# Layer 1's dt product from stacked half-precision halves, and the experts' middle one slot later

## What is computed

```
proj = hidden @ W_in.T;  x, gate = split(proj)           # 1024 channels each
x = silu(causal_conv(x, 4 taps))
ssm = x @ W_x.T;  ts, B, C = split(ssm, [32, 16, 16]);  each one RMS-normalised
dt = softplus(ts @ W_dt.T + b_dt)                        # the product that changes
state = state * exp(dt * A) + (dt * x) * B               # scan over the tokens, 16 states
y = (sum over states of state * C + x * D) * silu(gate)
x = x + ga * (y @ W_out.T)
# experts: base = h @ base_W.T; mid = (h @ lora_A) * w_top2; x = x + gb * (base + 2 * mid @ lora_B)
```

## Time and profile before

| | |
|---|---|
| median of three runs | 1513.37 us (1512.45 to 1514.31) |
| profiled execution, its own time | 1512.44 us |
| its span | 1510.3 us |
| PE, DVE, ACT, POOL busy share | 89%, 80%, 63%, 68% |
| instructions | 25293 |
| layer 1 in the span | from 489 us on |
| an iteration of layer 1 | 118.1 us |

### The profile page before, as it was taken

How to read it: one execution, slowest core, us unless ns; L and a number is a source line. 1 busy time by engine, 2 the same in 40 slices (tenths; PEclk the granted TensorE clock), 3 DMA queues, 4 the chain that set the end, 5 groups by cost and what they waited for, 6 DMA issues and landing times.

```text
span 1510.3 us, 25293 instructions
## 1 busy us (share of the span) xinstructions
PE 1349.8 (89%) x8817; PEld 1006.2 (67%) x8817; DVE 1213.1 (80%) x1643; ACT 952.1 (63%) x2617; POOL 1028.2 (68%) x697
## 2 busy tenths in 40 slices
PE   6899999999999959699899899899899999988677
PEld 5566677768776748568668667667766766855543
DVE  5794674556443469999999999999999999999994
ACT  3432343233321577788888897798798888886761
POOL 0353242313212398998998999899899899899870
PEclk9799999999999979899999999999999999999689
DMA  9531222101100200100110110020030020020001
GB/s 331 195 112 37 91 79 84 56 29 36 36 29 15 87 18 1 57 29 15 57 42 1 57 57 1 31 83 1 15 99 1 15 86 14 1 71 29 1 1 42
DMA packets 32388, 77.16 MB, mean 51 GB/s; under 512 B 3667, under 2 KB 4723, under 8 KB 31750
## 3 DMA queue, kind: packets, MB, share of 16 engines
q1 hardware_dynamic: 32262, 75.55, 15.1%
HBM read 66.99 MB, written 8.55 MB: 50 GB/s over the span
## 4 chain that ended last, share of the span: by engine, by line
PE 31%; POOL 13%; DVE 12%; ACT 6%; issue 5%; DVEq 0%; ACTq 0%; POOLq 0%
PE ps_h L1502 10%; DVE h L2273 7%; POOL h L2131 7%; POOL dbu L2097 6%; PE ps_m L1466 4%; DVE acc L2289 3%; ACT ps_a L1757 2%; PE ps_o L1526 2%; PE ps_m L165 2%; PE ps_s L1466 2%; PE ps_m L166 2%; PE ps_m L167 2%; PE ps_m L1426 2%; ACT ab L1889 1%; PE ps_s L165 1%
## 5 line engine op out<-in xcount | busy, mean ns | idle before, releaser
L2273 DVE TENSOR_TENSOR_SCAN h<-ps_a,dbu 128x512 f32<-128x512 f32 x512 | 595.8, 1205 | 21.3 <-ACT ps_a L1757 7.1
L2097 POOL TENSOR_TENSOR dbu<-dtu,b_all 128x1020 f32<-128x1020 f32 x256 | 598.3, 2358 | 14.4 <-DVE h L2273 13.9
L1757 ACT ACTIVATE ps_a<-dt,a_neg 128x256 f32<-128x256 f32 (+1 forms) x1024 | 442.9, 466 | 67.7 <-DVE h L2273 66.6
L1502 PE MATMUL ps_h<-ident,h 128*128 128x128 f32 x1536 | 226.4, 290 | 65.3 <-DVE acc L2289 60.0
L2289 DVE SCALAR_TENSOR_TENSOR acc<-ps_h,c_cur,acc 128x512 f32<-128x512 f32 x384 | 267.9, 737 | 16.9 <-PE ps_h L1502 16.3
L1502 PEld LDWEIGHTS ps_h<-ident,h 128*128 128x128 f32 x1536 | 183.1, 149 | 123.0 <-DVE h L2273 82.4
L724 POOL TENSOR_TENSOR hid_l<-hid,hid_h 128x256 f16<-128x256 f32 (+1 forms) x88 | 77.4, 883 | 155.0 <-ACT hid_h L610 154.8
L2131 POOL TENSOR_TENSOR h<-h,c_all 128x1024 f32<-128x1024 f32 x64 | 151.1, 2362 | 19.2 <-ACT carry L1777 19.2
L602 ACT ACTIVATE sil<-ps_gu 128x256 f32<-128x256 f32 (+1 forms) x88 | 33.9, 385 | 180.6 <-PE ps_gu L167 180.6
L165 PE MATMUL ps_m<-h_h,wi_h 128*128 128x256 f16 x432 | 119.4, 276 | 2.6 <-PEq L155 2.4
L166 PE MATMUL ps_m<-h_l,wi_h 128*128 128x256 f16 x432 | 119.2, 276 | 0.0
(11 more groups left out here) (406 smaller groups left out, 2876.8 us busy)
## 6 DMA issues: line engine op xcount, KB each, us to landing
b_all<-bt_scratch SPq DMA_DIRECT2D x32, 512.0 KB, 3.9
wm<-in_wmod SPq DMA_DIRECT2D x7, 1024.0 KB, 5.2
wo<-in_wmod SPq DMA_DIRECT2D x5, 1024.0 KB, 8.6
xa<-in_x SPq DMA_DIRECT2D x8, 512.0 KB, 4.5
stage<-in_W_in SPq DMA_DIRECT2D x4, 1024.0 KB
x_scratch<-x SPq DMA_DIRECT2D x8, 512.0 KB, 3.1
c_all<-bt_scratch SPq DMA_DIRECT2D x8, 512.0 KB, 6.0
x<-x_scratch SPq DMA_DIRECT2D x8, 512.0 KB, 3.6
```

Of the source, the lines that this page charges most:

```text
L1502: tr = pe.transpose(ps_h[:, t, j * P:(j + 1) * P], h[:, s % RING, j, t * P:(t + 1) * P], W["ident"][:])
L1757: ex = nc.scalar.activation(ps_a[:, j, j % 2:], dt[:, m, j % 2:], ACT.Exp, scale=a_neg[:, m, st:st + 1])
L2097: nc.gpsimd.tensor_tensor(dbu[:, s % AHEAD, :, 1:], dtu[:, :, 1:], b_all[:, st, 1:].unsqueeze(1).to_broadcast([P, DG, CH - 1]), ALU.mult). ...
L2273: nc.vector.tensor_tensor_scan(h[:, s % RING, two].rearrange("p j t -> p (j t)"), ps_a[:, two].rearrange("p j t -> p (j t)"), dbu[:, s % A ...
```

## The change

dt's product is made in half precision. Both factors are split in a high and a low half and stacked on the contraction axis: `w_dt` (scaled by WS = 64) has rows high, high, low of W_dt and high, low of b_dt; `ts` has rows high, low, high and ones. One half-precision matmul of 128x256 then gives the three products that the single-precision one stood for. For this `ssn` holds ts three times (`rms_apply` writes 192 instead of 64 elements), ACT copies all three to `ts` in slot 23, PE takes the high half from the middle rows in PSUM (`low_of_ts`, a new matmul by `minus_mid`, slot 23), and ACT copies the rest in slot 24: the low half, B and C to `tsb`, and `b0` (`ts_low_in`). So `spread_b` waits for a copy one slot later. The dt tiles stand four in slot 24 and four in slot 26, `dt_abs` takes four tiles in slot 25 and four in slot 27. `MID_AT` goes from 27 to 28 and `LB_AT` from 29 to 30. Before the loop, `w_dt` is made on chip: five DMAs instead of three, two ACT copies and one DVE operation more, and ACT's load of the table for ln moves behind `ts_low_in`.

```
-DT_AT = {23: (0, 1), 24: (2, 3), 25: (4, 5), 26: (6, 7)}
-MID_AT = 27
+DT_AT = {24: (0, 1, 2, 3), 26: (4, 5, 6, 7)}
+MID_AT = 28
-LB_AT = {29: (0, 1)}
+LB_AT = {30: (0, 1)}
...
-            pe.matmul(dt_bank(m), w_dt[:, m * P:(m + 1) * P], tsb[:], start=True, stop=True)\
+            pe.matmul(dt_bank(m), w_dt[:, m * P:(m + 1) * P], ts[:], start=True, stop=True)\
...
+        def low_of_ts(n):
+            pe.wait_ge(S["ts_done"], n * 2 + 1)
+            pe.matmul(ps_s[:, 0:CH], minus_mid[:], ts[:], start=False, stop=True, skip_group_check=True).then_inc(S["ts_sub"], 1)
...
         def tsb_in(n):
             act.wait_ge(S["tsb_mm"], n + 1)
-            nc.scalar.activation(tsb[0:RDT + NS + KC, :], ps_s[0:RDT + NS + KC, 0:CH], ACT.Copy).then_inc(S["tsb_done"], 1)
+            nc.scalar.activation(ts[0:BC0, :], ps_s[0:BC0, 0:CH], ACT.Copy).then_inc(S["ts_done"], 1)
+
+        def ts_low_in(n):
+            act.wait_ge(S["ts_sub"], n + 1)
+            nc.scalar.activation(ts[RDT:2 * RDT, :], ps_s[RDT:2 * RDT, 0:CH], ACT.Copy).then_inc(S["ts_done"], 1)
+            nc.scalar.activation(tsb[BC0:BC0 + NS + KC, :], ps_s[BC0:BC0 + NS + KC, 0:CH], ACT.Copy).then_inc(S["tsb_done"], 1)
             nc.scalar.activation(b0[:], ps_s[:, CH:CH + NS], ACT.Copy).then_inc(S["b0_done"], 1)
...
+            if m == 2:
+                act.wait_ge(S["w1_loaded"], 16 * 5)
+                nc.scalar.activation(w_dt[:], w_dt_in, ACT.Copy, scale=WS).then_inc(S["w_dt_made"], 1)
```

More of the change, by code:

```diff
@@ L1117, in layer_1 @@
     diag_t = sb("diag_t", [P, KI, TAPS, P], F32, c)
-    w_dt = sb("w_dt", [P, DI], F32, c)
+    w_dt = sb("w_dt", [P, DI], F16, c)
     hist = sb("hist", [P, KI, TAPS - 1], F32, c)
@@ L1278, in _ @@
         sp.wait_ge(S["pad_done"], 1)
-        sp.dma_start(w_dt[0:RDT, :], A["W_dt"]).then_inc(S["w1_loaded"], 16)
-        sp.dma_start(w_dt[ONE_ROW:ONE_ROW + 1, :], A["b_dt"]).then_inc(S["w1_loaded"], 16)
+        for at in range(3):
+            sp.dma_start(w_dt_in[at * RDT:(at + 1) * RDT, :], A["W_dt"]).then_inc(S["w1_loaded"], 16)
+        sp.dma_start(w_dt_in[ONE_ROW:ONE_ROW + 2, :], A["b_dt"].to_broadcast([2, DI])).then_inc(S["w1_loaded"], 16)
         def load_xa(n):
@@ L1452, in turn_tsb @@
             for t in range(TT):
-                pe.transpose(ps_s[0:RDT + NS + KC, t * P:(t + 1) * P], ssn[:, t, 0:RDT + NS + KC], W["ident"][:])
-            pe.matmul(ps_s[:, CH:CH + NS], W["ident"][:, 0:1].to_broadcast([P, P]), ssn[:, 0, RDT:RDT + NS], start=True, stop=True)\
+                pe.matmul(ps_s[:, t * P:(t + 1) * P], ssn[:, t, :], W["ident"][:], is_transpose=True, start=(t == 0), stop=False,
+                          skip_group_check=True)
+            pe.matmul(ps_s[:, CH:CH + NS], W["ident"][:, 0:1].to_broadcast([P, P]), ssn[:, 0, BC0:BC0 + NS], start=False, stop=True,
+                      skip_group_check=True)\
                 .then_inc(S["tsb_mm"], 1)
@@ L1664, in iteration @@
                 if n is not None:
+                    if s == TSB_AT + 1:
+                        low_of_ts(n)
                     for m in DT_AT.get(s, ()):
@@ L1717, in _ @@
         turn_tsb(0)
-        pe.wait_ge(S["w1_loaded"], 16 * 3)
+        pe.wait_ge(S["w_dt_made"], 5)
+        low_of_ts(0)
         for m in range(KI):
@@ L1868, in dt_abs @@
             top = dt[:, m:m + 2] if m < DG else relu[:, m - DG:m - DG + 2]
-            nc.scalar.activation(top, two, ACT.Relu)
-            nc.scalar.activation(ab[:, m:m + 2], two, ACT.Abs).then_inc(S["dt_abs"], 2)
+            nc.scalar.activation(top, two, ACT.Relu, scale=1.0 / WS)
+            nc.scalar.activation(ab[:, m:m + 2], two, ACT.Abs, scale=1.0 / WS).then_inc(S["dt_abs"], 2)
         def dt_decay(n, g):
@@ L1940, in keep_c @@
             act.wait_ge(S["ssn_done"], i * 2 + 2)
-            nc.scalar.activation(c_cur[:], ssn[:, :, RDT + NS:], ACT.Copy).then_inc(S["c_done"], 1)
+            nc.scalar.activation(c_cur[:], ssn[:, :, BC0 + NS:], ACT.Copy).then_inc(S["c_done"], 1)
         def join_acc(i, g, first):
@@ L2007, in others @@
                 tsb_in(n)
+            if n is not None and s == TSB_AT + 2:
+                ts_low_in(n)
             if n is not None:
@@ L2049, in _ @@
         nc.scalar.activation(minus[:], W["ident"][:], ACT.Copy, scale=-1.0).then_inc(S["nms_a"], 1)
-        act.wait_ge(S["nms_a"], 1)
+        act.wait_ge(S["nms_a"], 3)
+        act.wait_ge(S["w_dt_made"], 1)
+        nc.scalar.activation(minus_mid[RDT:2 * RDT, RDT:2 * RDT], minus[RDT:2 * RDT, RDT:2 * RDT], ACT.Copy).then_inc(S["w_dt_made"], 1)
         act.wait_ge(S["begun"], 1)
@@ L2056, in _ @@
                 x_tanh(0, m - 1, True)
+            if m == 2:
+                act.wait_ge(S["w1_loaded"], 16 * 5)
+                nc.scalar.activation(w_dt[:], w_dt_in, ACT.Copy, scale=WS).then_inc(S["w_dt_made"], 1)
+            if m == 6:
+                act.wait_ge(S["w_dt_made"], 4)
+                nc.scalar.activation(w_dt[ONE_ROW:ONE_ROW + 1, :], w_dt_in[ONE_ROW:ONE_ROW + 1, :], ACT.Copy, scale=WS)\
+                  .then_inc(S["w_dt_made"], 1)
         ss_in(0, True)
         squares(0)
-        act.wait_ge(S["w1_loaded"], 16 * 3)
+        act.wait_ge(S["w1_loaded"], 16 * 5)
         nc.scalar.activation(a_neg[:], a_neg[:], ACT.Exp).then_inc(S["nms_a"], 1)
         gate_tanh(0, 0)
-        nc.scalar.preload_act_table_set("natural_log_exp_and_others")
         act.wait_ge(S["begun"], 6)
         tsb_in(0)
+        ts_low_in(0)
+        nc.scalar.preload_act_table_set("natural_log_exp_and_others")
         for m in range(0, DG, 2):
@@ L2238, in iteration @@
                 others(i, p, n, first, s)
-        nc.gpsimd.memset(w_dt[:], 0.0).then_inc(S["pad_done"], 1)
+        nc.gpsimd.memset(w_dt_in, 0.0).then_inc(S["pad_done"], 1)
         for m in (4, 6, 5, 7):
@@ L2463, in _ @@
                 diagonals(m + 1)
+            if m == 2:
+                dve.wait_ge(S["w_dt_made"], 3)
+                nc.vector.scalar_tensor_tensor(w_dt[2 * RDT:, :], w_dt_in[2 * RDT:, :], WS, w_dt[2 * RDT:, :], ALU.mult, ALU.subtract)\
+                  .then_inc(S["w_dt_made"], 1)
         mean_squares(0)
```

27 lines of the change are left out of this document (17 added, 10 removed).

## The result

| | before | after |
|---|---|---|
| median | 1512.45 us (1510.95 to 1514.31, five runs) | 1541.26 us (1538.65 to 1542.36, five runs) |
| ratio to before | | 1.0182, 95% interval 1.0166 to 1.0197 |
| profiled execution, its own time | 1512.44 us | 1538.65 us |
| its span | 1510.3 us | 1536.7 us |
| mean granted clock | 0.959 | 0.943 |

The change costs 28.8 us by the medians and 26.2 us by the two profiled executions. The prediction was 1533 us, between 1519 and 1546.

What follows compares the result with a forecast made beforehand. It took DVE, fed by ACT one slot ahead, as the bound. Six iterations of 2.3 us lateness plus 1.15 for the clock, less 0.9 at the start, add 19.8 us: 1532.2 us profiled, median 1533, range 1519 to 1546.

Steps and rivals of the forecast that it cites:

- What bounds: Whole loop: DVE has no time left and ACT feeds it one slot ahead, so late exponentials cost DVE at once.
- The product, the copies, slot 25: Slots 22 to 27: PE's saving and the copies count 0, wider rms_apply 0 to 0.18 us, later exponentials cost 0.15 us.
- The three scans: DVE's scans of slots 30, 31 and the next 0 wait for ACT 1.5, 0.5 and 1.5 us more.
- The waits of ACT: ACT idles about 2 us before its mid_t copy, and its first base_out waits 1.8 us or more for lora.
- What is given back: Slots 0 to 7: DVE's waits of 1.09 us before add_state(4) and 0.3 recover 1.4 us; 2.3 of 3.65 stay.
- The clock: PE idles 3.5 us before turn_h(30); its clock falls in five of six iterations, 1.4 us each, 1.15 an iteration.
- The start, and iteration 0: Ahead of the loop, faster dt tiles less added work: -0.9 us, between -2 and +1.5; iteration 0 as before.
- The sum: Six iterations of 2.3 + 1.15 us less 0.9 at the start: 19.8 us more, 1532.2 us profiled, median 1533.
- the likeliest case: Late copies and lora, with the clock falling in most iterations: 1529 to 1540 us, chance 0.50.
- the rival in which nothing is given back: POOL is held up as long as DVE and the clock falls: 31.2 us more, 1545 us; chance 0.12.
- What was to show it: Signs: ACT's and DVE's waits, PE idle 3.5 us, transposes of 1.9 us, iterations of 121 to 122 us, 0 and 7 unchanged.
- a sign of being wrong: Named as refuting: mid_t without a wait, a period of 118 us, or one of over 123.

Runs made afterwards that it cites:

- slots back: The kernel after with MID_AT back at 27 and LB_AT back at 29, half-precision product kept: 1514.53 us, ratio 1.0005 to the kernel before.
- gap filled: The kernel after plus 14 zero-weight half-precision matmuls behind turn_h(29) in iterations 1 to 6: 1532.99 us, ratio 1.0135 to the kernel before.
- slots alone: The kernel before with only MID_AT 28 and LB_AT 30, product still single precision: 1541.33 us, ratio 1.0184.
- slots 22 and 23 kept busy: The kernel after with MID_AT 27, LB_AT 29 and zero matmuls added, 7 in slot 22 and 8 in slot 23: 1516.53 us, ratio 1.0028.
- middle later: The kernel after with LB_AT back at 29, MID_AT still 28, turn_mid behind the gate tiles: 1521.95 us, ratio 1.0056 to the kernel before.
- both ahead of the gates: The kernel after, slots as changed, but turn_mid (slot 28) and lora (slot 30) called ahead of their gate tiles: 1521.76 us, ratio 1.0052.
- `lora` later: The kernel after with MID_AT back at 27, LB_AT still 30, lora behind gate tile 4: 1523.83 us, ratio 1.0066 to the kernel before.

## Why the prediction was right, and where its sizes were off

**What bounds.** Right: DVE, fed by ACT one slot ahead. With the slots back, sixteen single-precision records an iteration became eight short ones without an effect that can be told.

**The product, the copies, slot 25.** The saving was taken at 0 and is 0, to the 0.2% that can be told. `rms_apply` takes 0.36 us instead of 0.23, 0.13 of the 0.18 allowed. Slot 25 was to cost 0.15 us and costs 0.17:

```profile
997.48 2.34 DVE L2304 TENSOR_TENSOR_SCAN h<-ps_a,dbu 128x512 f32<-128x512 f32 x2 [0.17 <-ACT carry L1791]
```

**The three scans.** Predicted 1.5, 0.5 and 1.5 us with the clock apart; measured 1.63, 0.42 and 1.53. The waits of ACT were predicted at about 2 us for `mid_in` (2.10) and 1.8 for `base_out` (1.84 where the clock held). PE's idle time was to be 3.5 us and is 3.67. In sum 3.65 predicted, 3.75 measured.

**What is given back.** This is the term that was mis-sized most: 1.4 us predicted, 0.8 measured (3.75 - 2.97). The prediction took DVE's whole wait of 1.09 us before `add_state(4)` and 0.3 for the weighed states. The first was right: the row that stood at 1029.89 with a wait of 1.09 us has none now.

```profile
1042.15 1.39 DVE L2320 SCALAR_TENSOR_TENSOR acc<-ps_h,c_cur,acc 128x512 f32<-128x512 f32 x2
```

The second did not come back at all: DVE's wait for the weighed states is 0.27 us in each of iterations 1 to 6, before and after. In iteration 2 the first wait was 1.01 us before; less the 0.13 that `rms_apply` adds, that is 0.88, near the 0.8 measured. POOL was seen rightly as the reason for giving back, and a little too good: the prediction had it 1.75 us less late than DVE (1.9 against 3.65). It began to weigh state 0 at 1011.36, 4.23 us after scan 0' began; now

```profile
1023.32 2.37 POOL L2162 TENSOR_TENSOR h<-h,c_all 128x1024 f32<-128x1024 f32 x1 [4.16 <-ACT carry L1791]
```

that is 2.78 us after scan 0' (1020.54), and it has waited for that scan's carry, so 1.45 us less late than DVE and no more.

**The clock.** Predicted: it falls in five of six iterations at 1.4 us each, 7 us. It fell in five of six. Four of the falls cost 1.46, 1.50, 1.65 and 1.67 us (waits for scan 0' of 2.99, 3.03, 3.18 and 3.20 less the 1.53 of iteration 2), and one, in iteration 1, 2.76, where the clock stayed at 0.50 for six us (below); 9.0 us together. The kernel with the gap filled gives 8.3 us by the medians, which is the same term measured in another way. So the error is 2 us. Iteration 1, as a row of the same columns as above:

```profile
768.00:774.00 6.00, 6.00 (x23) 4.38 (x24) 4.15 (x5) 1.70 (x5) 6.00 (x3) 0.50 0.00 0
```

The page "TensorE: Matmul & The Clock Gate" of the Trainium skill, on HAM oscillation, would have had the fall in every iteration. The trace disagrees in detail: after 3.66 us of idle time one of six held here, and none of six in the kernel with the slots alone.

**The start, and iteration 0.** Predicted -0.9 us, in a range of -2 to +1.5, and the start itself gives -0.8: DVE's wait for the softplus, 7.75 us before, is 6.95 now, and 6.94 in the kernel with the slots back.

```profile
523.84 1.23 DVE L2412 TENSOR_TENSOR dt<-dt,ab 128x1024 f32<-128x1024 f32 x1 [6.95 <-ACT ab L1896]
```

But iteration 0, which was to be as before, uses it up. From its first scan to the `sg` row of iteration 1 it takes 125.25 us (529.16 to 654.41) instead of 124.29 (530.52 to 654.81). Of these 0.96 us 0.17 are slot 25; the rest is not explained. It seems to come with the product and not with the slots: seven of the eight kernels with the half-precision product take 125.2 to 126.0 us there (the eighth, with slots 22 and 23 kept busy, 124.6), the one with the slots alone 124.45.

**The sum.** The waits give 6 x 2.97 = 17.8 us where 13.8 were predicted (4.0 more, nearly all of it the give-back), and the clock 9.0 for 6.9 (2.1 more). The periods show another 0.6, in iteration 1, for which no wait was found. That is 27.4 us. Outside of these six the sum is -1.0: -0.55 ahead of the dt tiles, which is less than layer 0 differs between executions (below), -0.8 at the start, +0.96 in iteration 0 and -0.6 behind the last `sg` row. That it is so near the predicted -0.9 is partly luck. Together it is the 26.4 us of the spans, against 19.8. The forecast was the likeliest case and its mechanism the measured one; by size the result lies between it (1533 us) and the rival in which nothing is given back (1545 us). The medians' distance, 28.8 us, is 2.6 more than that of the profiled executions, since the profiled one of after is the fastest of its five.

**What was to show it.** The wait of `mid_in`, those of scans 30 and 31, that of `base_out` (1.84 us or more) and PE's idle time before `turn_h(30)` are there in all six iterations. The transposes behind it take 1.94 us in two of them and 1.57 to 1.70 in three, since the clock fell only in their course; at full clock they take 1.22 behind such a gap. The period was to be 121 to 122: it is 121.1 once, 122.6 to 122.7 four times, and 124.7 in iteration 1, which lies beyond the 123 that were named as a sign of being wrong. Iteration 0 is not as before (above).

## What to carry to other kernels

When a step moves by a slot, look at what it now stands behind in its engine's stream and at what stands behind its consumer: here a copy of 0.38 us that waited 2.1 us for PE delayed the exponentials behind it, and the engine that bounds paid for it. Putting such a step ahead of the bulk work of its slot cost nothing for the middle (1.0005), behind it 1.0056; for `lora`, which was late by its slot too, it helped little (1.0052, against 1.0066 behind the gate tile). Slack can be spent once: add up delays first and subtract what is given back from the sum, and add the clock's price wherever the delay opens a gap in front of work that someone waits for.

## What the runs showed of the hardware

**The same gap has two outcomes.** Whether the granted clock fell within five us behind the start of `turn_h(30)`, by PE's idle time ahead of it, six iterations each:

| idle time, us | kernel | fell |
|---|---|---|
| 0.64 | gap filled | 0 of 6 |
| 1.95 | middle later | 0 of 6 |
| 1.94 | both ahead of the gates | 4 of 6 |
| 2.15 | `lora` later | 1 of 6 |
| 3.67 | after | 5 of 6 |
| 3.66 | slots alone | 6 of 6 |

The idle time by itself doesn't decide it; what else does was not tested. Nor does a burst at full speed right behind a gap show that the clock has held: in two iterations of the kernel with the slots alone the transposes took 1.22 us after 3.66 us of idle time, the fall came behind them, and scan 0' waited 3.2 us all the same.

**Zero matmuls are enough to hold it.** 3.19 us of half-precision matmuls with zero weights in a gap of some 3.7 us kept it at 2.4 GHz in six of six iterations. The idle time that was left ahead of `turn_h(30)` was 0.64 us.

**Layer 0 doesn't take the same time in every execution.** The same early row of DVE, in the trace of after and in that of the kernel with the slots back, whose code is the same up to there:

```profile
516.07 0.69 DVE L2356 SCALAR_TENSOR_TENSOR sg<-th,ps_m 128x512 f32<-128x512 f32 x1 [0.41 <-ACT th L1865]
...
520.39 0.69 DVE L2356 SCALAR_TENSOR_TENSOR sg<-th,ps_m 128x512 f32<-128x512 f32 x1 [0.41 <-ACT th L1865]
```

4.3 us apart, more than most of the effects in question. The stretch behind the last `sg` row differs as much from trace to trace, 144.2 to 148.9 us over the ten kernels. The periods of the loop repeat better: before, the six lie within 0.3 us of one another, and five of the kernel with `lora` alone within 0.04. So an effect in the loop is better read from the periods than from two spans. Where that offset comes from is open.
